# Two small on-chip tiles change places between the root frame and the frame of the first phase

## The reference

```python
# layer 0
h = relu(layernorm(x));  q, k = split(h @ Wqk);  v = h @ Wv
w = (1/sqrt(512)) * mask * sum_d(q * (adj @ k))          # one number for each node
x = x + softmax(w over the nodes)[:, :, None] * v
# layer 1
h = relu(layernorm(x));  q, k, v = h @ Wq.T + bq, h @ Wk.T + bk, h @ Wv.T + bv
w = adj * exp(q @ k.T);  x = x + (w / w.sum(-1)) @ v
# layer 2: 8 heads of 64
h = relu(layernorm(x));  s = (q @ k.T) / 8 * (adj + adj)
x = x + (softmax(s) @ v) @ Wo.T + bo
# layer 3
h = relu(layernorm(x));  Xw = h @ Wv + bv
a = adj * exp(leaky_relu(Xw @ aw[:d] (of j) + Xw @ aw[d:] (of i) + ab));  T = a / (a.sum(-1) + 1e-12)
x = x + relu(sum over k of (T^k h) @ Wk[k] + bk[k]), k = 0, 1, 2
```

## Time and profile before

| | |
|---|---|
| median of 3 executions | 2437.03 us |
| the profiled execution's own time | 2437.03 us |
| its span, from the first to the last instruction | 2435.1 us |
| PE busy | 2363.6 us (97%) |
| DVE, POOL and ACT busy | 55%, 35% and 34% |
| granted clock of PE, mean | 0.99 |

### The profile page before, as it was taken

One profiled execution on the slowest core, in us unless ns is written; L12 is line 12 of the kernel. 1 busy time (PEld: TensorE's weight loads), 2 busy tenths in 40 slices (PEclk: granted clock), 3 DMA queues, 4 the chain that ended last, 5 costly groups with the idle time before them and its releaser, 6 DMA issues.

```text
span 2435.1 us, 39821 instructions
## 1 busy us (share of the span) xinstructions
PE 2363.6 (97%) x16095; PEld 1932.4 (79%) x16095; DVE 1335.6 (55%) x2572; ACT 818.1 (34%) x1493; POOL 846.5 (35%) x1040
## 2 busy tenths in 40 slices
PE   7899999999999999999999999999789999999998
PEld 4688888888888887888888888888678888887877
DVE  2566555566556544445544455444666666665653
ACT  2344343334333333333333333333322222323221
POOL 2355445445545423233322333222441313131221
PEclk9899999999999999999999999999899999999999
DMA  5222333232333333222322223112332222223221
GB/s 169 68 81 74 88 100 92 81 85 74 82 89 107 90 111 100 57 57 71 99 58 57 57 72 98 57 57 83 102 92 72 89 73 86 77 75 88 71 72 38
DMA packets 152057, 197.98 MB, mean 81 GB/s; under 512 B 61936, under 2 KB 62016, under 8 KB 151872
## 3 DMA queue, kind: packets, MB, share of 16 engines
q1 hardware_dynamic: 151872, 195.42, 28.1%
HBM read 77.90 MB, written 50.33 MB: 53 GB/s over the span
## 4 chain that ended last, share of the span: by engine, by line
PE 71%; DVE 7%; issue 7%; POOL 6%; SPq 5%; ACT 3%; DMA 1%; ACTq 0%; DVEq 0%; POOLq 0%
PE bank L313 31%; PE bank L303 28%; SPq L1441 5%; POOL h3T_lo L1221 3%; PE bank L329 3%; PE bank L375 2%; DVE hs L665 2%; DVE stA L644 2%; ACT hn L980 1%; PE bank L522 1%; PE bank L495 1%; PE bank L293 1%; PE bank L505 1%; DVE yt L939 1%; POOL stA L1211 1%
## 5 line engine op out<-in xcount | busy, mean ns | idle before, releaser
L313 PE MATMUL bank<-w_hi,h3T_hi 128*128 128x512 f32 x768 | 304.1, 396 | 0.0
L313 PE MATMUL bank<-w_hi,h3T_lo 128*128 128x512 f32 x768 | 299.5, 390 | 0.0
L313 PE MATMUL bank<-w_lo,h3T_hi 128*128 128x512 f32 x768 | 299.5, 390 | 0.0
L633 DVE TENSOR_TENSOR Z_lo<-bank,Z_hi 128x512 fp32r<-128x512 f32 x128 | 82.9, 685 | 216.9 <-ACT Z_hi L966 216.9
L980 ACT ACTIVATE hn<-x,stA 128x512 f32<-128x512 f32 x192 | 140.7, 804 | 145.1 <-POOL stA L1213 144.1
L1208 POOL TENSOR_SCALAR stA<-stA 128x4 f32<-128x4 f32 x48 | 11.6, 242 | 485.7 <-DVE stA L646 485.6
L313 PEld LDWEIGHTS bank<-w_hi,h3T_lo 128*128 128x128 f32 x768 | 144.4, 188 | 30.4
L313 PEld LDWEIGHTS bank<-w_lo,h3T_hi 128*128 128x128 f32 x768 | 144.7, 188 | 29.8
L313 PEld LDWEIGHTS bank<-w_hi,h3T_hi 128*128 128x128 f32 x768 | 144.8, 189 | 29.5
L665 DVE STREAM_TRANSPOSE hs<-hn 128x512 f32<-128x512 f32 x192 | 123.9, 688 | 74.1 <-ACT hn L980 74.1
L633 DVE TENSOR_TENSOR cT_lo<-bank,cT_hi 128x256 fp32r<-128x256 f32 x128 | 44.8, 411 | 206.2 <-ACT cT_hi L966 206.2
(11 more groups left out here) (246 smaller groups left out, 6165.6 us busy)
## 6 DMA issues: line engine op xcount, KB each, us to landing
hGA<-hs SPq DMA_DIRECT2D x768, 64.0 KB, 2.0
mid<-x SPq DMA_DIRECT2D x32, 1024.0 KB, 4.6
x<-mid SPq DMA_DIRECT2D x32, 1024.0 KB, 5.7
x<-in_x SPq DMA_DIRECT2D x16, 1024.0 KB, 6.0
hGB<-hs SPq DMA_DIRECT2D x256, 64.0 KB, 2.0
out<-x SPq DMA_DIRECT2D x16, 1024.0 KB, 4.9
abf<-in_adj SPq DMA_DIRECT2D x64, 64.0 KB, 5.1
adj<-in_adj SPq DMA_DIRECT2D x64, 64.0 KB, 3.3
```

What stands on the lines that cost most here:

```text
L313: ins = eng.matmul(b[:], h[l][:, k, ts], W[r][:, k, :], start=(k == 0 and i == 0), stop=(last and k == 3 and i == 2))
L633: return eng.tensor_tensor(lo, src, hi.bitcast(F), ALU.subtract)
```

## The change

`stA` is allocated in `root`, where `ecol` was, and `ecol` in phase A's frame, where `stA` was. `pad2` and `pad5` are each 32 floats smaller.

```diff
         mhalf, cst, abc, s0 = (small[:, i:i + 1] for i in range(4))
-        ecol = [alloc(root, f"ecol{i}", [128, 8]) for i in range(2)]
-        stB = alloc(root, "stB", [128, 4, 12])
+        stA, stB = alloc(root, "stA", [128, 4, 12]), alloc(root, "stB", [128, 4, 12])
         late = stB[:].rearrange("p t n -> p (t n)")
...
         ucol, wS, pcol, rcol = (cols[:, i:i + 4] for i in range(0, 16, 4))
-        stA = alloc(pa, "stA", [128, 4, 12])
+        ecol = [alloc(pa, f"ecol{i}", [128, 8]) for i in range(2)]
         tmp = ExitStack()
...
-        alloc(pb, "pad2", [128, 928])
+        alloc(pb, "pad2", [128, 896])
         hT2.append(pair(pb, "h2T1"))
...
-        alloc(pc, "pad5", [128, 160])
+        alloc(pc, "pad5", [128, 128])
         hT3.append(pair(pc, "h3T1"))
```

## The result

The changed kernel takes 2456.46 us (median of 4, 2455.72 to 2459.28) against 2437.2 us before (median of 4): the ratio is 1.008, with a 95% interval of 1.0062 to 1.0098. I had forecast no difference, with 6 in 100 for slower, and 1 of them for a slower pace of PE. The profiled span is 2455.0 us, 19.9 more than before.

What follows compares the result with a forecast made beforehand. PE was taken to bound the kernel. The sum was 2435.1 us of span + 0 (`stA`) + 0 (`ecol`) + 0 (shift) + 1.93 around the span = 2437.03 us, with a range of 2434 to 2442 us.

Steps and rivals of the forecast that it cites:

- What bounds the kernel: Whole kernel: PE, busy 2363.6 of 2435.1 us; only its pace or its 71.5 us of standing still counts.
- the place where slack is short: Layer 3, L586: PE waits for `sib` 15 times, 17.3 us in all, the longest sum of waits.
- The ring of layer 3: Layer 3, from statistics in `stA` to `sib` and PE: 20.1 us a turn; additions lengthen PE's wait in 15 groups.
- The move of `stA` and `ecol`: New addresses of both tiles: 0 each; for `stA` bounds of 1.5 us down and 3.6 us up.
- The shift, for DVE, ACT, POOL and the transfers: Tiles starting 128 bytes higher: 0; bounds either side 1.3 us for the engines, 0.4 us for transfers.
- the rule on fetched beats: Gathers out of `hs`: 66 beats instead of 70, landing at most 0.11 us sooner, 0.5 us over four gathers.
- The rival: PE's 512-column matmuls: shifted operands change its pace, one cycle on 9,024, 3.8 us either way; chance 0.02, half each side.
- 0 (shift): Term of the sum for tiles starting 128 bytes higher: 0 us added to the span.
- three signs of being wrong: L586's wait moving over 5 us, a PE pace changing half a nanosecond, PE standing still in layers 0 and 1's loop.
- Collisions: Layer 3's ring, DVE's long durations: entering, up to 16.9 us slower, chance 0.05; leaving, 5.9 us faster, chance 0.03.
- as many long ones as before: Profile after, L954 and L941: same medians and the same number of long durations.

Runs made afterwards that it cites:

- all-even kernel: Changed kernel with pads of phases B and C resized and `cols`, `ecol` behind phase A's last tile, all distances multiples of 256 bytes: 2435.72 us, ratio 0.9992.

## Why the prediction was wrong

- **What bounds the kernel** was right, and so was the place where slack is short. The ring of layer 3 explains why 1,344 of the 4,800 slow matmuls cost almost nothing. I had looked at it only from the side of the engines that feed it, where an addition counts in full; from PE's side it is a cushion of 17.3 us.
- **The move of `stA` and `ecol`** at 0 was right: in the all-even kernel both have moved and the ratio is 0.9992.
- **The shift, for DVE, ACT, POOL and the transfers**, at 0 was right. L818 on `sm` spreads over 685 to 690 ns, `al` and `tt` take 738 and 734. The gathers still land after 2.0 us, 1,992 ns in the median before and 1,994.5 after; the 1.9 us that I had tied to the rule on fetched beats are not in the trace. But one level down, in the records of the single packets, the source's offset shows. The 2,048-byte packets of gathers with no other transfer beside them take 136.3 ns in the mean before (source 192 bytes past a multiple of 256), 129.5 after (source at 64) and 130.4 in the kernel with all tiles 64 bytes lower (source at 128); the target plays no part, as `hGA` and `hGB` give the same. My step from there to a shorter landing failed: packets 7 ns shorter didn't move the 2.0 us. The Trainium skill, "DMA: Bandwidth & Descriptors", section "How a descriptor splits into AXI transactions", has a descriptor fetch from the 256-byte boundary below its start, which made 66 beats out of 70, 6% less (an estimate); the packets' 5% agree with it.
- **The step that failed** is in the same part: "For PE no row shows the moving operand of a 128x512 matmul at another offset, so the shift's price on its pace is a rival below." The rival got 2 in 100 and was sized at one cycle, 3.8 us, for which no row spoke. The true price is 4.8 to 6.4 ns on 4,800 matmuls. By the table's differences that is 9.1 us in layer 1, 10.1 in layer 2 and 8.0 in layer 3 (with the even groups' 0.6 ns), 27.2 us; measured by stages it is 9.0, 11.1 and 7.7 of the 29.4 us by which PE is busier. So the term "0 (shift)" of the sum held for every engine but PE, for which it had no row. I left that unknown cost out of the range, where it belonged: with the one instruction class that fills 97% of the span, a price without a row has no bound.
- The argument against the rival was upside down. "Half of the tiles of layer 2 and 3 don't shift at all" was exactly what costs. I asked what an offset does to an operand, and never what the difference of two offsets does to an instruction that reads both.
- I had named three signs of being wrong, and two came: the pace of PE changed by more than half a nanosecond (q2 of odd groups went from 10.89 to 11.20 us), and the wait at `sib` moved by more than 5 us, from 17.3 to 10.3. The second follows from the first. PE doesn't stand still longer in the loop of layers 0 and 1.
- **Collisions** in and out of the ring did not come about: L953 and L940, the lines that were L954 and L941, still have medians of 684 and 692 ns, and their sums are unchanged (84.9 us; 50.2 and 50.3). Only the forecast of as many long ones as before fails for L940, where 10 of 64 last over 1 us, and 15 did.

What stays open: by what mechanism two reads at unequal offsets hinder each other. The loads of stationary operands run beside the matmuls, and that the price follows from the difference of the two offsets and its direction (229 or 233 ns) speaks for a meeting of the two streams, without showing it. Whether the moving operand meets the stationary one of its own matmul or the one that is loaded for the next wasn't told apart. That the slow pace outlasts its cause tells nothing of it. In layer 3's even groups only the three T by Z1 matmuls of a tile are uneven, and the five or so even ones after them run at 228 to 236 ns too; but before the change, with equal offsets throughout, such intervals follow on short matmuls too.

## What to carry to other kernels

Before a change of layout, list the start offsets, modulo 256 bytes, of the two operands of each hot matmul, and keep the pairs equal; a pad or a few small tiles at the other end of a frame do it. An address is a parameter like a size: where the bounding engine's instructions would read from a combination that the trace doesn't hold, its price is unknown, not zero, and the count of those instructions says how wide the range must be. Where an engine waits at a fixed place in each turn, part of a slowdown of that engine is free, and only there.

## What the runs showed of the hardware

A 128 by 512 matmul of rounded float32 operands, back to back with others of its kind and with a granted clock of 1.00, starts every 227 ns when stationary and moving operand begin at the same offset modulo 256 bytes, whichever it is (64, 128 and 192 were tried). At the other seven distances in steps of 32 bytes it starts every 232 to 234 ns, but for one: a moving operand 64 bytes above (or 192 below) the stationary one, 229 ns. Behind short matmuls the first few start at intervals of up to 236 ns, also where all offsets are equal. The Trainium skill, "SBUF — State Buffer", section "Who interferes with whom", calls TensorE's two read ports independent and says that TensorE never waits on anyone. What was measured is that the addresses of its own two operands change its pace by 2 to 3%, 19 us in this kernel, with no more idle time in the profile; whether the two ports are where it happens isn't shown.

The packets of an on-chip gather of 2,048-byte runs take 136 ns in the mean from a source 192 bytes past a multiple of 256, and 130 from 64 or 128 past one, while the time from issue to landing stays at 2.0 us.
